# Cross-attention and FFN kernel: batch 0's row maxima from f32 projections by 32-row matmuls, without the way through DRAM

## The reference

```python
def attention(query, key, value, mask, w_q, w_k, w_v, w_o):
    Q = (query @ w_q.T).reshape(b, tgt, 16, 8).transpose(0, 2, 1, 3)
    K = (key @ w_k.T).reshape(b, src, 16, 8).transpose(0, 2, 1, 3)
    V = (value @ w_v.T).reshape(b, src, 16, 8).transpose(0, 2, 1, 3)
    scores = jnp.einsum('bhtd,bhsd->bhts', Q, K) / np.sqrt(8)
    scores = jnp.where(mask[:, None, None, :], scores, -jnp.inf)
    attn = jax.nn.softmax(scores, axis=-1)
    out = jnp.einsum('bhts,bhsd->bhtd', attn, V)
    return out.transpose(0, 2, 1, 3).reshape(b, tgt, d) @ w_o.T

def ffn(x, w_gate, w_up, w_down):
    gate, up = x @ w_gate.T / 127, x @ w_up.T / 127
    return (jax.nn.silu(gate) * up) @ w_down.T / 127

x = x + attention(layernorm(x), ctx_1024, ctx_1024, mask, w_q, w_k, w_v, w_o)
x = x + ffn(layernorm(x), w_gate, w_up, w_down)
```

## Time and profile before

| | |
|---|---|
| median of 3 runs | 191.45 us (189.88 to 256.48) |
| profiled execution | 189.59 us, of which the span of the trace is 187.8 us |
| PE busy | 168.6 us (90%) in 1636 matmul records |
| DVE, ACT, POOL busy | 133.3 us (71%), 107.2 us (57%), 67.0 us (36%) |
| chain that ended last | PE 54%, DVE 17%, issue 15%, POOL 6% |
| DMA | 17.06 MB in 17381 packets |

### The profile page before, as it was taken

One profiled execution on the slowest core, in us unless ns is written; L12 is line 12 of the kernel. 1 busy time (PEld: TensorE's weight loads), 2 busy tenths in 40 slices (PEclk: granted clock), 3 DMA queues, 4 the chain that ended last, 5 costly groups with the idle time before them and its releaser, 6 DMA issues.

```text
span 187.8 us, 4293 instructions
## 1 busy us (share of the span) xinstructions
PE 168.6 (90%) x1636; PEld 105.9 (56%) x1636; DVE 133.3 (71%) x308; ACT 107.2 (57%) x226; POOL 67.0 (36%) x114
## 2 busy tenths in 40 slices
PE   5858998599996999999999999998999999997883
PEld 4648554254452556557656655754565466655863
DVE  6853897676799578968896886899689815425441
ACT  5432014657794488577867785777577577533030
POOL 6233605918427533950674085004100500310100
PEclk9996999659999699999999999999999999999999
DMA  4739797491096029405930870394000000000100
GB/s 147 261 97 183 210 179 231 134 185 24 8 245 94 3 63 213 68 0 155 173 47 12 232 133 0 93 212 67 3 30 2 3 2 28 5 28 0 31 2 28
DMA packets 17381, 17.06 MB, mean 91 GB/s; under 512 B 1520, under 2 KB 15984, under 8 KB 16688
## 3 DMA queue, kind: packets, MB, share of 16 engines
q1 hardware_dynamic: 16896, 16.12, 37.4%
q10 hardware_dynamic: 464, 0.67, 1.3%
HBM read 9.24 MB, written 7.34 MB: 88 GB/s over the span
## 4 chain that ended last, share of the span: by engine, by line
PE 54%; DVE 17%; issue 15%; POOL 6%; ACT 3%; DMA 2%; ACTq 1%; SPq 1%; POOLq 0%
PE pv_bank L336 12%; PE score_bank L276 9%; DVE neg_max L742 9%; PE pv_bank L403 5%; PE max_bank L293 4%; PE ffn_bank L389 4%; PE ffn_bank L377 3%; DMA ctx_all<-ctxT 2%; PE ffn_bank L380 2%; PE prep_bank L315 2%; PE prep_bank L307 2%; PE post_bank L365 2%; PE post_bank L352 2%; DVE stats L811 1%; PE prep_bank L311 1%
## 5 line engine op out<-in xcount | busy, mean ns | idle before, releaser
L742 DVE TENSOR_REDUCE neg_max<-max_bank 128x2 f32<-128x512 f32 x128 | 82.0, 685 | 17.9 <-PE max_bank L293 17.3
L566 ACT ACTIVATE probs<-score_bank 128x512 f32<-128x512 f32 x128 | 70.0, 597 | 20.7 <-PE score_bank L276 20.7
L293 PE MATMUL max_bank<-k_ops,q_ops 49*128 49x256 bf16 x256 | 44.0, 280 | 2.8 <-DVE neg_max L742 2.8
L276 PE MATMUL score_bank<-q_ops,k_ops 51*128 51x256 bf16 x256 | 43.7, 280 | 1.9 <-ACT probs L566 1.1
L336 PE MATMUL pv_bank<-probs,v_ops 128*32 128x256 f32 x512 | 35.2, 390 | 0.0
L276 PEld LDWEIGHTS score_bank<-q_ops,k_ops 51*128 51x128 bf16 x256 | 19.8, 95 | 22.1 <-ACT probs L566 9.9
L293 PEld LDWEIGHTS max_bank<-k_ops,q_ops 49*128 49x128 bf16 x256 | 17.4, 95 | 8.3 <-DVE neg_max L742 5.6
L990 POOL CAST max_parts<-neg_max 128x16 bf16<-128x16 f32 x14 | 2.8, 198 | 51.7 <-DVE neg_max L742 51.7
L336 PEld LDWEIGHTS pv_bank<-probs,v_ops 128*32 128x32 f32 x512 | 14.7, 110 | 11.2 <-issue 5.4
L403 PE MATMUL pv_bank<-ident_bf 128*128 128x128 bf16 x212 | 18.5, 242 | 1.9 <-POOL ident_bf L1020 1.9
L403 PEld LDWEIGHTS pv_bank<-ident_bf 128*128 128x128 bf16 x212 | 15.0, 110 | 5.9 <-issue 3.6
(11 more groups left out here) (117 smaller groups left out, 221.0 us busy)
## 6 DMA issues: line engine op xcount, KB each, us to landing
k_ops<-k_rows SPq DMA_DIRECT2D x7, 384.0 KB, 4.8
q_ops<-q_rows SPq DMA_DIRECT2D x7, 384.0 KB, 6.1
k_rows<-kq_parts SPq DMA_DIRECT2D x8, 192.0 KB, 2.1
q_rows<-kq_parts SPq DMA_DIRECT2D x8, 192.0 KB, 2.2
k_rows<-kq_parts SPq DMA_DIRECT2D x8, 128.0 KB, 2.1
q_rows<-kq_parts SPq DMA_DIRECT2D x8, 128.0 KB, 2.1
out<-y SPq DMA_DIRECT2D x8, 128.0 KB, 2.1
x_all<-x SPq DMA_DIRECT2D x1, 768.0 KB, 6.6
```

Source lines behind the costliest of these rows:

```text
L276: mm = pe.matmul(score_bank[k % 2][:, t * S:(t + 1) * S], rows(k_ops, b, ROWS)[:, k, t * P:(t + 1) * P], rows(q_ops, b, ROWS)[:, k, :], st ...
L293: mm = pe.matmul(max_bank[k % 2][:, t * S:(t + 1) * S], rows(q_ops, b, MAX_ROWS)[:, k, t * P:(t + 1) * P], rows(k_ops, b, MAX_ROWS)[:, k, ...
L566: act.activation(probs[:, k % RING].rearrange("p t s -> p (t s)"), score_bank[k % 2][:, :], ACT.Exp, scale=SCALE).then_inc(probs_ready, 1)
L742: dve.tensor_reduce(neg_max[:, b % 2, :, k], max_bank[k % 2][:, :].rearrange("p (t s) -> p t s", t=TT), AX.X, ALU.max, negate=True).then_i ...
```

## The change

Batch 0's maxima are no longer formed from the split bf16 operands that come back from DRAM, but from f32 Q and K directly:

- DVE makes a second copy of the K and Q weights with other column order (`w_heads`), so that a projection (`project_for_heads`) puts the 8 rows of four heads into each group of 32 partitions. Head k has group k % 4 and place k // 4 in it.
- ACT writes the K projection four times into `k_heads`, each time scaled by a column of `head_rows` that is 1 on the rows of one place and 0 on the others, and copies Q once (`q_heads`). A matmul over the 32 rows of a group then gives one head's scores.
- `first_max_scores` runs for each head and each half of the queries an f32 matmul over 32 rows and a bf16 matmul over one row (ones by `mask0`, the mask bias of batch 0, loaded on all partitions). It uses four PSUM banks in turn.
- The dummies between heads, and the 40 ahead of them, go. In their place the heads are mixed with the preparation of batches 0 to 2.
- Batch 0's split operands still go through DRAM, for `scores(0, ...)`, now in one piece for each side. `scores(0, 0)` waits for them and for all 16 maxima.
- Order: SP sends `ctx_all[:, 2:4]` after `spread_shift(0, 0)` and the integer FFN weights after that; `ctx_all[:, 0]` moves to ACT's list; ACT fills `k_ops[1]` after `copy_kq(2)`, POOL fills `q_ops[1]` (DVE before), and `root_of_x(3)` comes after `fill_v(2)`.

The diff, without the declarations:

```diff
-            sp.dma_start(ctx_all[:, 0], ctxT[:, 0]).then_inc(ctx_in[0], 16)
...
-            sp.wait_ge(q_filled[0], 1)
-            sp.wait_ge(q_bounced[0], 16 * PARTS)
-            for g in range(2):
-                half_from_dram(sp, 0, g)
-            sp.dma_start(ctx_all[:, 2:4], ctxT[:, 2:4]).then_inc(ctx_in[2], 16)
             for part, done in enumerate((k_part1, k_part2, k1_part3)):
                 sp.wait_ge(done, 1 if part == 2 else 2)
                 to_dram(1, 1, part)
+            sp.wait_ge(q_filled[0], 1)
+            from_dram(sp, 0, 0)
...
+            spread_shift(0, 0)
+            sp.dma_start(ctx_all[:, 2:4], ctxT[:, 2:4]).then_inc(ctx_in[2], 16)
             sp.dma_start(wff_int[:, :, :], wff_in).then_inc(wff_loaded, 16)
-            spread_shift(0, 0)
...
+            def first_max_scores(k):
+                if k == 0:
+                    pe.wait_ge(q_heads_ready, 1)
+                    pe.wait_ge(ones_ready, 1)
+                    pe.wait_ge(mask0_ready, 1)
+                    pe.wait_ge(k_heads_ready, 1)
+                if k == 3:
+                    pe.wait_ge(k_heads_ready, OF_GROUP)
+                if k >= 4:
+                    pe.wait_ge(max_done, k - 3)
+                r = GROUP * (k % 4)
+                to = first_max_bank[k % 4]
+                for t in range(TT):
+                    pe.matmul(to[:, t * S:(t + 1) * S], q_heads[r:r + GROUP, t * P:(t + 1) * P],
+                              k_heads[r:r + GROUP, k // 4], start=True, stop=False)
+                    mm = pe.matmul(to[:, t * S:(t + 1) * S], ones_row[r:r + 1, :], mask0[r:r + 1, :],
+                                   start=False, stop=True)
+                mm.then_inc(max_scores_ready, 1)
...
             pe.wait_ge(ident_ready, 2)
-            keep_warm(18, pv_bank)
+            keep_warm(18, max_bank[0])
             pe.wait_ge(wkq_loaded, 16)
-            project_k(0, score_bank[0][:, 0:S]).then_inc(k_proj, 1)
-            project_k(1, max_bank[0][:, 0:S]).then_inc(k_proj, 1)
-            keep_warm(16, pv_bank)
-            turn_xn1(0, score_bank[1])
-            keep_warm(6, pv_bank)
+            ctx_wait(pe, 0)
+            project_for_heads(0, score_bank[1][:, 0:S], ctx_all[:, 0]).then_inc(k_heads_proj, 1)
+            project_k(0, pv_bank[:, 0:S]).then_inc(k_proj, 1)
+            project_k(1, prep_bank[:, 0:S]).then_inc(k_proj, 1)
+            keep_warm(8, max_bank[0])
+            turn_xn1(0, score_bank[0])
+            keep_warm(6, max_bank[0])
+            pe.wait_ge(xn1_t_ready, 1)
+            project_for_heads(1, post_bank[:, 0:S], xn1_t[:, :]).then_inc(q_heads_proj, 1)
             project_q(0, ffn_bank[:, 0:S]).then_inc(q_proj, 1)
-            project_q(1, score_bank[1][:, 0:S]).then_inc(q_proj, 1)
-            pe.wait_ge(v_ready, 1)
-            project_v(1, post_bank)
-            keep_warm(40, pv_bank)
-            pe.wait_ge(k_rest, 2)
-            for k in range(HEADS):
-                max_head(0, k)
-                keep_warm(4, pv_bank)
...
+            keep_warm(4, max_bank[0])
+            first_max_scores(0)
+            turn_xn1(1, post_bank)
+            first_max_scores(1)
+            first_max_scores(2)
+            project_q(1, post_bank[:, 0:S]).then_inc(q_proj, 1)
+            first_max_scores(3)
...
+            first_max_scores(8)
+            turn_xn1(2, pv_bank)
+            first_max_scores(9)
+            first_max_scores(10)
             pe.wait_ge(q_rest, 2)
+            turn_max(0, 0, post_bank)
+            first_max_scores(11)
+            first_max_scores(12)
+            pe.wait_ge(xn1_t_ready, 3)
+            project_k(2, pv_bank[:, 0:S])
+            project_q(2, pv_bank[:, S:2 * S]).then_inc(kq_proj, 1)
+            first_max_scores(13)
+            first_max_scores(14)
+            first_max_scores(15)
...
             fill_q(0)
-            fill_q(1)
+            dve.wait_ge(ident_ready, 1)
+            dve.tensor_reduce(head_rows[:, :], ident[:, :].rearrange("p (g j d) -> p j g d", j=OF_GROUP, d=DK), AX.XY,
+                              ALU.max).then_inc(head_rows_ready, 1)
+            dve.wait_ge(wkq_loaded, 16)
+            for side in range(2):
+                dve.tensor_copy(w_heads[:, side].rearrange("p (g j d) -> p g j d", j=OF_GROUP, d=DK),
+                                wkq[:, side].rearrange("p (d j g) -> p g j d", d=DK, j=OF_GROUP))\
+                    .then_inc(w_heads_ready, 1)
...
-            stats_of_x(2)
-            moments_of_x(2)
-            eps_of_x(2)
-            rest(1, q_part1, score_bank[1][:, 0:S], kq_f, S, q_rest)
+            for k in range(HEADS):
+                head_max(0, k)
+                if k == 1:
+                    rest(1, q_part1, post_bank[:, 0:S], kq_f, S, q_rest)
+                if k == 3:
+                    stats_of_x(2)
+                if k == 4:
+                    moments_of_x(2)
+                    eps_of_x(2)
+                if k == HALF - 1:
+                    parts_of_max(0, 0)
+            parts_of_max(0, 1)
             stats_of_x(3)
```

142 lines of the change are left out of this document (81 added, 61 removed).

## The result

The changed kernel takes **204.2 us** (median of 4 runs, 204.0 to 205.0) where the kernel before takes 191.4 on the same chip: ratio 1.071, 95% interval 1.064 to 1.078. It is slower by 12.8 us. The forecast was 193.5, with a range up to 198. The profiled execution took 204.01 us, its span is 202.2 (before 187.8). Some executions of most of these kernels show a lower granted clock than the others of the same kernel and take over 1.5% longer; the ratios leave them out, so a ratio need not be that of the medians.

A forecast was written before the change was run, and what follows sets the result against it. Bound: how early batch 2 is projected, plus 8.34 us of ACT and POOL behind it. 189.6 + 2.8 (later `kq_f` copy) + 0.7 (POOL's root) = 193.1, put at 193.5 because the profiled execution was under the median; range 187.5 to 198.

The forecast's parts named there:

- Start of the heads: Prologue on PE: head 0 of batch 0's maxima starts at about 12.9 us, 6.4 us earlier than 19.28.
- first reduction: DVE, batch 0's maxima: head 0's reduction at 15.8 to 16.9 us, against 19.71 before.
- The clock through the maxima: PE, batch 0's maxima: full clock, since PE is hardly idle between 9.4 and 26 us; low clock given 0.22.
- The overlap of heads: PE, batch 0's maxima: neighbouring heads overlap fully, so each of 6 runs of heads takes 1.1 us.
- Rival C: PE, batch 0's maxima: no overlap between groups, at full clock, max_t 2.6 us later, 195.7 us; chance 0.12.
- B and C together: PE, batch 0's maxima: low clock and no overlap, everything doubles, max_t at 43 us, about 210 us in all.
- B: PE, batch 0's maxima: clock stays at 1.2 GHz, five runs of heads cost 2.2 us each, 197.6 us; chance 0.22.
- T: Time when max_t, for the first half of batch 0's shift, is ready: 24.9 to 26.0 us, against 27.39.
- the transfer: SP's context of batches 2 and 3, behind the shift: lands 3.5 to 4.6 us later, PE waits some 3.5 us.
- K: Start of ACT's `kq_f` copy after batch 2's projections: 32.0 us (30.2 to 33.4), 2.8 later than 29.21.
- POOL's root in the chain: POOL, behind the `kq_f` copy: `root_of_x(3)`, before done in an idle time, now adds 0.73 us.
- Nothing gives a late start back: Loop after the turn of xn(3), 37.55 us before: close weave of PE, DVE and ACT, same distances as before.

The follow-up runs named there:

- the late execution: Profiled execution of the changed kernel with all edits, 4 dummies, shift first and FFN weights late; it took 203.7 us, the kernel's median was 188.4 us.

## Why the prediction was wrong, step by step

**Start of the heads, first reduction: right.** Head 0 at 12.35 (12.9 forecast), first reduction at 15.37, 0.4 ahead of the 15.8 to 16.9. `head_rows` and the weight copies cost nothing.

**The clock through the maxima: the step that failed.** I forecast full clock and gave the low one 0.22, "against it: PE is hardly idle between 9.4 and 26". PE was not idle at all there, and the clock of 14 to 26 was 1.00 up to about 18 and 0.50 from then on. My argument took busy time as what the clock asks for; the runs show that the rows in use count too. With PE busy for 14.00 of 14 us the clock is 0.50 with 32 rows in the maxima and 1.00 with 128, and twelve dummies of 32 rows leave it at 0.50 (208.3 us) where those of 128 rows hold it at 1.00 (198.3 us). The Trainium skill, TensorE: Matmul & The Clock Gate, Part 1: The HAM clock gate, explains the clock by how busy PE has been; by that alone the clock should have stayed up, and the measurement decides against so plain a reading. A row that could have warned me is in the earlier trace rows, where the clock fell with a PE that was busy for 3.16 of 4 us on 49 and 51 rows; I quoted it and gave it little weight. The price of the rival, 197.6, was too small as well: it counted five runs of heads at the low clock and left the turns, projections and the first batch at full clock, while the clock stayed at 0.50 up to 55.

**The overlap of heads: wrong in size.** I took 1.1 us for any run. In the change's order a run of n heads takes about n + 1 halves of 0.54 us, at the low clock of 1.02, and a head by itself 1.28 (12.35 to 13.63). Rival C (no overlap) was wrong too; the truth lies between. B and C together were priced at 210, and 204.2 lies between B and that. The Trainium skill, same page, Part 3: Packing small matmuls — row/col tiling, has the matmuls start strictly in program order. At 14.54 head 2 starts 0.11 us ahead of the second f32 matmul of head 1, which precedes it in the program, so the rule as it stands is not what the trace shows. But what I concluded from the earlier trace rows, full overlap in whatever order the matmuls stand, was further off: each head waited for most of a half of its neighbour, and putting the matmuls of different groups side by side gave 2.0%.

**T, the transfer and K.** The shift was issued at 32.38 (24.9 to 26.0 forecast), late through the two points above. Behind it the mechanism was right: transfer issued right behind the shift, 4.24 us to landing (3.5 to 4.6), idle time 2.21 us ended by it (some 3.5 forecast). K was 39.7, 7.7 later than the 32.0 forecast. As a term of its own, in the kernel before, the late transfer costs 5.3 us, more than the whole forecast of 3.5 for K and POOL; in its trace the clock falls behind the pause.

**POOL's root in the chain: not on the path.** I had added 0.7 for it. It waited for DVE's variance (1.02 us) and still was in time: heads 13 to 15 at half clock, 39.64 to 44.1, and the first scores were later. The turn of xn(3) had no idle time before it.

**Nothing gives a late start back: right.** In seventeen traces, all but that of the late execution, the span less the turn's start lies between 149.1 and 152.6 us (before 150.3, after 152.2), while the turn itself moves from 35.42 to 55.94. What remains of the spread goes with the clock behind the turn: its mean there is 0.96 to 0.97 where the rest takes over 152 us, and 0.98 to 0.99 elsewhere.

**The sum.** Of the 12.8 us, full-height dummies give back 4.7 although they cost some 0.7 us at each of eight places; the order of the heads 4.1; the context 1.7 alone and 2.7 on top of the dummies; all of it together, with xn(3) and the first reduction, 13.5. The parts aren't additive, so no share is given for each. With order and context mended the dummies are worth 7.2 us (1.037 against 0.999), more than alone; that the clock is the largest part of the 12.8 is what this suggests, not what it shows.

**What the idea could be worth.** The maxima start 7 us earlier, and nothing of that is seen at the end even when everything is mended. Of the 5.7 us at the first reduction 1.0 is left at the last one, and then the shift's place on SP and ACT's weights are next. With ACT's weights moved in both kernels the old way through DRAM is as fast, and its times were steadier.
